# The reciprocal deviations of four normalisations: a power on GpSimd in place of a root on ScalarE and a reciprocal on VectorE

## The chip, the cores and the metric

The kernel runs on one core of a Trainium2 chip. The metric is the device time of one execution in microseconds, the median of the timed runs. The core's engines work side by side, each on its own queue in program order, and wait for each other by semaphores: PE (TensorE), VectorE (DVE), ScalarE (ACT), GpSimd (POOL) and SyncE (SP), which issues most of the DMAs.

## The reference

Two transformer layers with modulated normalisation, on x of 16 x 256 tokens (4096 in all) of width 128. In each layer, with six modulation vectors made from c:

    h = layernorm(x) * (1 + ca) + sa;  x = x + ga * attention(h)
    h = layernorm(x) * (1 + cb) + sb;  x = x + gb * feedforward(h)
    layernorm(x) = (x - mean) / sqrt(var + 1e-5), over the 128 features

The first layer's attention is a linear state-space scan with 16 states; its feed-forward is a mixture of 8 experts, two for each token, computed densely with rerouting by a similarity matrix. The second layer has causal attention with 16 heads, rotary embedding and relative positions; its feed-forward is a shared expert plus two of eight experts for each token, of hidden width 512. So there are four normalisations, numbered 0 to 3.

## The kernel before

The 4096 tokens are 32 tiles of 128 rows (`NT`), four tiles are a chunk of 512 (`NC` = 8 chunks), which is two sequences. X stays in SBUF for the whole kernel. Every engine has its instruction list written out by hand in the order in which it is to work; there is no planner. A wait at the head of an engine's list holds everything behind it.

A normalisation goes so: VectorE makes mean and variance of a chunk into `MV` (`statistics`, L1020, semaphore `s_mv`); ScalarE makes the deviation `SD` as `Sqrt(var + EPS)` (`s_sd`); VectorE takes the reciprocal into `RSTD`; then each tile is shifted and scaled, PE transposes it and ScalarE or VectorE applies the modulation into `hT`.

- Normalisation 0 (start): VectorE interleaves `first_statistics` and `normalise0` (L1064 to L1078); ScalarE makes six deviations before the first `features0`. After it VectorE makes the gates `GG`, which are stored and loaded again, broadcast, and GpSimd adds the attention's constant part to X (L652).
- Normalisation 1 (around 48 to 99 us): PE makes `outputs(c)` and, from c = 3, `transposes0(1, c - 3)` in turn (L1739). VectorE's loop (L1141) does `gated(c)`, `statistics(c - 1)`, `scales0(c - 2)`; GpSimd adds the residual between the first two. Here ScalarE normalises:

```python
            for c in range(NC):
                deviation(1, c)
                if c >= 2:
                    normalise1st(c - 2)
                if c >= 3:
                    features0(1, c - 3)
```

- Normalisation 2 (around 276 to 311 us): it follows the last expert pass of the first layer. For each chunk GpSimd makes a product with the gate (two halves, L675) and adds it to X (L679), VectorE makes the statistics behind it. One `Sqrt` over all 32 tiles (L769) and one reciprocal (L1102) follow, then `normalise(2)`.
- Normalisation 3 is spread over the second attention's eight pairs of sequences. `statistics1(i - 2)` comes at the end of pair i on VectorE. ScalarE makes the deviations in three lots: chunks 0 to 4 at the start of the last pair, 5 and 6, and 7 (L907); VectorE takes the reciprocals in the same lots (L1406) before `normalise1(0)`, `normalise1(5)` and `normalise1(7)` (L1394).

After the attention comes the tail, from about 660 to 815 us. For each of four groups of two chunks VectorE chooses the experts (`choose`) and computes destinations (`destinations`), and GpSimd scatters the rows with 16 indirect DMAs (L741). Beside that PE works through the shared expert (`shared_up`, `shared_down`), and VectorE adds its results (`shared_out`). The end of VectorE's list is: `destinations(2)`, `last_context(7)`, `shared_out(0)`, `gate_out(7)`, `last_residual(7)`, `statistics1(7)`, `shared_out(1)`, reciprocal, `normalise1(7)`, `shared_out(2)`, `choose(3)`, `shared_out(3)`, `destinations(3)`. PE's list has `norm_transposes(7)` behind `shared_up(3)`, then `shared_down(2)`, the router for chunk 7, and the rest of the shared blocks: `shared_up` 4 to 7 and `shared_down` 3 to 7. The routed experts' 39 tiles start when the shared expert and all scatters are done.

GpSimd's list in full: constant addition, residuals of layer 0 attention, a memset of `ACC`, the residuals of normalisation 2, rotary sums and low parts (L686, L691), for each pair `context`, `residual1` and copies (`neighbours`), then the four groups of scatters, then the results' scatters.

Of the kernel before, what the change touches and what calls it, by code (L numbers as in the profile page):

```python
# [19 lines left out]
ALU = mybir.AluOpType  # L20
# [3 lines left out]
P = 128  # L24
# [49 lines left out]
def build(nc, A, out):  # L74
    ctx = ExitStack()
    with ctx:
        def sb(name, shape, dt=F32):
            return ctx.enter_context(nc.sbuf_tensor("sb_" + name, shape, dt))
# [21 lines left out]
        MV = sb("MV", [P, NT, 2])  # L100
        RSTD = sb("RSTD", [P, NT])
        SD = sb("SD", [P, NT])
        NB = sb("NB", [P, NT])
        XN = sb("XN", [P, 2, TPC, D])
        epsc = sb("epsc", [P, 1])
        TMP = sb("TMP", [P, 2, CH])
# [179 lines left out]
        s_set = sem("s_set")  # L286
        s_cm = sem("s_cm")
        s_mod = sem("s_mod")
        s_gg = sem("s_gg")
        s_gst = sem("s_gst")  # L290
        s_gld = sem("s_gld")
        s_dv = sem("s_dv")
        s_mv = sem("s_mv")
        s_sd = sem("s_sd")
        s_xn = sem("s_xn")
# [349 lines left out]
        def _(pool):  # L645

            nc.gpsimd.memset(ones[:, :], 1.0).then_inc(s_set, 1)
            pool.wait_ge(s_vb, 16)
            pool.wait_ge(s_xn, NC)
# [12 lines left out]
            for c in range(NC):  # L662
                residual(c, c)
            nc.gpsimd.memset(ACC[:, :, :], 0.0).then_inc(s_zero, 1)
            pool.wait_ge(s_zero, 1)
# [3 lines left out]
            for c in range(NC):  # L669
                pool.wait_ge(s_acc[0], (E - 1) * NC + c + 1)  # L670
                t4 = TMP[:, c % 2, :].rearrange("p (b t f) -> p b t f", b=2, t=2)
                a4 = ACC[:, c * TPC:(c + 1) * TPC, :].rearrange("p (b t) f -> p b t f", b=2)
                for b in range(2):
                    gate = GATE[:, 1, 2 * c + b, :].unsqueeze(1).to_broadcast([P, 2, D])
                    ins = nc.gpsimd.tensor_tensor(t4[:, b], a4[:, b], gate, ALU.mult)  # L675
                ins.then_inc(s_gt0, 1)
                pool.wait_ge(s_gt0, c + 1)
                xs = X[:, c * TPC:(c + 1) * TPC, :].rearrange("p t f -> p (t f)")
                nc.gpsimd.tensor_tensor(xs, xs, TMP[:, c % 2, :], ALU.add).then_inc(s_r0, 1)  # L679

# [37 lines left out]
            for i in range(NP):  # L719
                if i == NP - 1:  # L720
                    nc.gpsimd.memset(RT1[32:33, :, :], 1.0).then_inc(s_one, 1)
                    pool.wait_ge(s_one, 1)
                if i >= 2:
                    context(i - 2)
                    residual1(i - 2)
                neighbours(i)
                pool.wait_ge(s_nb, 2 * i + 2)
            context(NP - 2)
            residual1(NP - 2)

            pool.wait_ge(s_pad, 16 * (E + 1))
            for g in range(GROUPS):
                pool.wait_ge(s_ids, 1 + (g > 0))
                pool.wait_ge(s_rows, 2 * GC * (g + 1))
# [25 lines left out]
        def _(act):  # L761
# [3 lines left out]
            def layer_norm(n, then=None):  # L765

                l, first = n // 2, 3 * (n % 2)
                act.wait_ge(s_mv, (n + 1) * NC)
                nc.scalar.activation(SD[:, :], MV[:, :, 1], ACT.Sqrt, bias=epsc[:, :]).then_inc(s_sd, 1)  # L769
                for c in range(NC):  # L770
# [9 lines left out]

            def deviation(n, c):
                act.wait_ge(s_mv, n * NC + c + 1)
                ts = slice(c * TPC, (c + 1) * TPC)
                nc.scalar.activation(SD[:, ts], MV[:, ts, 1], ACT.Sqrt, bias=epsc[:, :]).then_inc(s_sd, 1)

            def features0(n, c):
# [7 lines left out]

            for c in range(6):
                deviation(0, c)
            act.wait_ge(s_md, 1)
            features0(0, 0)
            features0(0, 1)
            deviation(0, 6)  # L800
            features0(0, 2)
            deviation(0, 7)
            def steps0(h):
# [30 lines left out]
            for c in range(NC):  # L834
                deviation(1, c)
                if c >= 2:
                    normalise1st(c - 2)
                if c >= 3:
                    features0(1, c - 3)
# [63 lines left out]
            exponentials(0)  # L903
            def deviations(n, lo, hi):
                act.wait_ge(s_mv, 3 * NC + hi)
                ts = slice(lo * TPC, hi * TPC)
                nc.scalar.activation(SD[:, ts], MV[:, ts, 1], ACT.Sqrt, bias=epsc[:, :]).then_inc(s_sd, 1)  # L907

            for i in range(1, NP):
                if i == NP - 1:  # L910
                    deviations(3, 0, 5)
                values_out(i - 1)
                relative_out(i - 1)
                exponentials(i)
# [43 lines left out]
            relative_out(NP - 1, (0,))  # L958
            deviations(4, 5, 7)
            shares(1)  # L960
# [10 lines left out]
            for c in range(3):  # L971
                shared_hidden(c)
            deviations(5, 7, 8)
            shared_hidden(3)
# [34 lines left out]
        def _(dve):  # L1009
# [18 lines left out]

            v.memset(epsc[:, :], EPS)
            for i in range(8):  # L1030
                link(v.memset(bank[i][:, :], 0.0))
            def normalise0(n, c):
                dve.wait_ge(s_sd, n * NC + c + 1)
                ts = slice(c * TPC, (c + 1) * TPC)
                link(v.reciprocal(RSTD[:, ts], SD[:, ts]))
                wait(dve, s_tr, n * NC + c - 1)
# [6 lines left out]
            def scales0(c):  # L1043
                dve.wait_ge(s_sd, NC + c + 1)
                ts = slice(c * TPC, (c + 1) * TPC)
                link(v.reciprocal(RSTD[:, ts], SD[:, ts]))
                v.scalar_tensor_tensor(out=NB[:, ts], in0=MV[:, ts, 0], scalar=-1.0, in1=RSTD[:, ts],
                                       op0=ALU.mult, op1=ALU.mult).then_inc(s_nbm, 1)
# [51 lines left out]
            def normalise(n, then=None):  # L1100
                dve.wait_ge(s_sd, n + 15)
                link(v.reciprocal(RSTD[:, :], SD[:, :]))  # L1102
                for c in range(NC):
                    wait(dve, s_tr, n * NC + c - 1)
                    for t in range(TPC):
# [287 lines left out]

            def normalise1(c):  # L1394
                if c >= 2:
                    dve.wait_ge(s_tr, 3 * NC + c - 1)
# [4 lines left out]
                ins.then_inc(s_xn, 1)  # L1401

            def inverse_deviations(n, lo, hi):
                dve.wait_ge(s_sd, n + 15)
                ts = slice(lo * TPC, hi * TPC)
                link(v.reciprocal(RSTD[:, ts], SD[:, ts]))  # L1406

            def last_pair(i, k):
# [6 lines left out]
                row_maxima(i, 1)  # L1415
                inverse_deviations(3, 0, 5)
                dve.wait_ge(s_wm[1], 16 * 11)
# [135 lines left out]
            statistics1(6)  # L1553
            inverse_deviations(4, 5, 7)
            normalise1(5)
# [13 lines left out]
            shared_out(1)  # L1569
            inverse_deviations(5, 7, 8)  # L1570
            normalise1(7)
# [725 lines left out]
```

## Time and profile before

| | before |
|---|---|
| median of 3 timed runs | 961.08 us (956.97 to 962.22) |
| span of the profiled execution | 1008.9 us |
| time of the profiled execution beside its span | none is given |
| PE busy | 838.6 us (83%) |
| VectorE busy | 592.7 us (59%) |
| ScalarE busy | 371.3 us (37%) |
| GpSimd busy | 255.6 us (25%) |
| mean granted TensorE clock | 0.890 of full |

The profile is of one execution, and its span is longer than the timed median. Times in it count from the first instruction. An engine is busy while one of its instructions executes, not while it waits. The chain is the work that ended last, followed back from the end through what released each step. Engines are named there PE, PEld (weight loads), DVE, ACT, POOL and SP; PEclk is the granted TensorE clock as a share of full.

### The profile page before, as it was taken

The numbers are of one execution on the slowest core, as the hardware profiler recorded it, in microseconds if no ns is written. First come the engines' busy times: TensorE is split into PE (matmuls) and PEld (weight loads), VectorE is DVE, ScalarE is ACT, GpSimd is POOL, SyncE is SP. The second block draws the span as 40 slices with busy tenths as digits, with TensorE's granted clock in tenths as the row PEclk, the third lists the DMA queues.
The fourth block names the chain that finished last, engine by engine and source line by source line (L and its number), as shares of the span: only waits on it lengthen the run. The fifth ranks groups of instructions, "written<-read, shape, count | busy, mean of one in ns | idle before, by whom it ended". The sixth has DMA issues, their size and how long they took to land.

```text
span 1008.9 us, 22593 instructions
## 1 busy us (share of the span) xinstructions
PE 838.6 (83%) x8710; PEld 572.5 (57%) x8710; DVE 592.7 (59%) x1638; ACT 371.3 (37%) x719; POOL 255.6 (25%) x252
## 2 busy tenths in 40 slices
PE   5545698999958789999999999986679789999960
PEld 3443365656634446656656656553257578888850
DVE  8632866666688787687687687763245232222217
ACT  3335221222214105435435436553325324444424
POOL 0522000000073601012011112034661514444440
PEclk9956699999989958999999999997688779999985
DMA  5600022226414761133233332121310417777746
GB/s 147 268 3 0 1 92 92 92 92 211 140 49 140 233 174 48 29 95 89 46 94 60 74 94 62 31 59 34 86 41 9 131 55 213 212 220 215 212 130 223
DMA packets 107827, 108.37 MB, mean 107 GB/s; under 512 B 48892, under 2 KB 93644, under 8 KB 106796
## 3 DMA queue, kind: packets, MB, share of 16 engines
q1 hardware_dynamic: 103196, 97.82, 33.7%
q0 software_dynamic: 4544, 9.35, 2.6%
q8 instruction: 60, 0.98, 0.4%
q14 instruction: 27, 0.22, 0.1%
HBM read 82.15 MB, written 44.78 MB: 126 GB/s over the span
## 4 chain that ended last, share of the span: by engine, by line
PE 62%; DVE 18%; issue 7%; ACT 5%; POOL 3%; DMA 3%; SPq 2%; POOLq 0%; DVEq 0%; ACTq 0%
PE bank L2148 8%; PE bank L2158 7%; PE bank L1928 7%; PE bank L1762 5%; PE bank L1773 5%; PE bank L1774 4%; PE bank L1868 4%; DVE sb_arena L1360 4%; PE bank L2077 3%; PE bank L1820 3%; PE bank L2067 3%; PE bank L1846 3%; DVE sb_ST L1023 2%; DVE sb_arena L1350 2%; DVE sb_arena L1352 2%
## 5 line engine op out<-in xcount | busy, mean ns | idle before, releaser
L1360 DVE TRANSPOSE_TENSOR_REDUCE sb_arena<-bank 128x16 f32<-128x512 f32 x192 | 120.3, 685 | 25.4 <-PE bank L1868 24.2
L901 ACT ACTIVATE sb_arena<-bank 128x512 f32<-128x512 f32 x192 | 99.2, 602 | 50.0 <-PE bank L1868 50.0
L989 ACT ACTIVATE sb_arena<-bank,sb_arena 128x256 f32<-128x256 f32 x156 | 65.3, 471 | 99.9 <-PE bank L2148 99.1
L749 POOL DMA_INDIRECT expert_results<-sb_arena x78 | 74.7, 958 | 105.5 <-DVE sb_arena L1619 88.9
L1762 PEld LDWEIGHTS bank<-sb_arena 128*128 128x128 f32 x512 | 67.9, 195 | 42.1 <-issue 25.3
L858 ACT ACTIVATE sb_arena<-bank 128x512 f32<-128x512 f32 x64 | 38.2, 597 | 143.9 <-PE bank L1774 143.8
L2148 PE MATMUL bank<-sb_arena 128*128 128x256 f32 x312 | 80.3, 402 | 3.8 <-DVE sb_arena L1615 1.8
L1928 PE MATMUL bank<-sb_arena 128*16 128x128 f32 x1024 | 71.9, 422 | 9.5 <-issue 9.4
L1762 PE MATMUL bank<-sb_arena 128*128 128x128 f32 x512 | 70.2, 281 | 10.5 <-DVE sb_arena L1192 10.5
L741 POOL DMA_INDIRECT dispatched_rows<-sb_arena x64 | 63.0, 984 | 62.7 <-DVE sb_arena L1525 44.4
L2158 PE MATMUL bank<-sb_arena 128*128 128x128 f32 x624 | 75.9, 275 | 0.0
L1254 DVE SCALAR_TENSOR_TENSOR sb_arena<-bank,sb_arena 128x128 f32<-128x128 f32 x256 | 71.7, 343 | 2.0 <-PE bank L1762 2.0
L2158 PEld LDWEIGHTS bank<-sb_arena 128*128 128x128 f32 x624 | 72.8, 192 | 0.1
L1192 DVE TENSOR_TENSOR sb_arena<-sb_arena,bank 128x512 f32<-128x512 f32 x64 | 43.7, 685 | 49.6 <-ACT sb_arena L858 49.0
L1773 PE MATMUL bank<-sb_arena 128*128 128x512 f32 x128 | 69.0, 622 | 0.0
L1774 PE MATMUL bank<-sb_arena 128*128 128x512 f32 x128 | 67.5, 609 | 0.0
L2148 PEld LDWEIGHTS bank<-sb_arena 128*128 128x128 f32 x312 | 58.3, 197 | 15.5 <-issue 5.3
L1820 PE MATMUL bank<-sb_arena 128*128 128x56 bf16 (+1 forms) x512 | 62.2, 281 | 5.5 <-DVE sb_arena L1340 3.2
L1350 DVE CAST sb_arena<-bank 128x512 bf16<-128x512 f32 x64 | 43.7, 682 | 37.0 <-PE bank L1820 37.0
L1613 DVE CAST sb_arena<-sb_arena 128x2 uint32<-128x2 f32 x39 | 7.8, 200 | 97.9 <-DMA expert_results<-sb_arena 81.3
L1868 PE MATMUL bank<-sb_arena,sb_identb 128*32 128x128 bf16 (+1 forms) x2304 | 63.1, 242 | 0.4 <-DVE sb_arena L1350 0.4
L1846 PE MATMUL bank<-sb_arena 32*128 32x256 bf16 x512 | 52.9, 285 | 6.8 <-DVE sb_arena L1360 4.5
(263 smaller groups left out, 1356.5 us busy)
## 6 DMA issues: line engine op xcount, KB each, us to landing
sb_arena<-in_w SPq DMA_DIRECT2D x39, 578.0 KB
dispatched_rows<-in_padding SPq DMA_DIRECT2D x8, 2064.0 KB, 9.5
sb_arena<-dispatched_rows SPq DMA_DIRECT2D x39, 129.0 KB
sb_arena<-q_parts SPq DMA_DIRECT2D x8, 512.0 KB, 5.5
sb_arena<-k_parts SPq DMA_DIRECT2D x8, 512.0 KB, 7.0
context_rel<-sb_arena SPq DMA_DIRECT2D x256, 8.0 KB
sb_arena<-expert_results SPq DMA_DIRECT2D x16, 256.0 KB, 5.9
q_parts<-sb_arena SPq DMA_DIRECT2D x24, 128.0 KB, 2.4
```

Source lines behind the costliest of these rows:

```text
L749: nc.gpsimd.indirect_dma_start(yD[:, :], bass.IndirectOffsetOnAxis(ap=rid[:, k, r:r + 1], axis=0), YS[:, k, r, :], None).then_inc(s_yo[k], 16)
L901: nc.scalar.activation(dst, src, ACT.Exp).then_inc(s_ex, 1)
L1360: v.tensor_reduce(dst.rearrange("p h b -> p (h b)"), bank[r % RING][:, :].rearrange("p (b c) -> p b c", c=32), AX, ALU.max, apply_transpos ...
L1762: ins = mm(bank[4 + j % 2][:, t * D:(t + 1) * D], HM0[:, j % 2, t * P:(t + 1) * P], W0[:, k, 2 * F0:3 * F0], start=True, stop=True)
L1773: mm(bank[j % 2][:, :], W0[:, k, 0:F0], chunk(hT, c), start=True, stop=True)
L1774: mm(bank[2 + j % 2][:, :], W0[:, k, F0:2 * F0], chunk(hT, c), start=True, stop=True).then_inc(s_up[0], 1)
L1820: ins = mm(out[:, :, :, x], GT4[:, first:first + 32, :].rearrange("p x a -> p (x a)"), queries[:, :, :, q], start=True, stop=True, skip_gr ...
L1846: mm(dst[:, x * S:(x + 1) * S], KG[k][rows, g, 0:P], QG[k][rows, g, :], start=(x == 0), stop=False, skip_group_check=True)
L1868: ins = mm(dst[32 * b:32 * b + 32, :, 32 * b:32 * b + w], identb[:, 32 * a:32 * a + 32], src[:, :, :].rearrange("p (g b) q -> p g b q", g= ...
L1928: ins = mm(out[32 * j:32 * j + 2 * HD, :, x], relk[:, 32 * j + 8 * w + 2 * x:32 * j + 8 * w + 2 * x + 2, :], four, start=True, stop=True, ...
L2148: ins = mm(bank[2 * (k % 2) + b // 2][:, b % 2 * GT:(b % 2 + 1) * GT], W1[:, k, b * P:(b + 1) * P], XT[:, k % 2, :], start=True, stop=True ...
L2158: ins = mm(bank[6 + k % 2][:, r * D:(r + 1) * D], HMT[:, k % 2, b, r * P:(r + 1) * P], W1[:, k, I1 + b * D:I1 + (b + 1) * D], start=(b == ...
```

## The change

The deviations leave ScalarE and the reciprocals leave VectorE. GpSimd computes, per chunk of four tiles, `SD = var + EPS` and then `RSTD = SD ** -0.5` with a tile of constants. VectorE's `inverse_deviation` is now only the wait for it. Normalisations 2 and 3 go by single chunks instead of lots. In GpSimd's queue the pairs stand behind the work that is shown here; the waits are part of that queue.

```diff
+            nc.gpsimd.memset(mhalf[:, :], -0.5).then_inc(s_half, 1)
+            pool.wait_ge(s_half, 1)
+            def inverse_deviation(n, c):
+                pool.wait_ge(s_mv, n * NC + c + 1)
+                ts = slice(c * TPC, (c + 1) * TPC)
+                nc.gpsimd.tensor_scalar(SD[:, ts], MV[:, ts, 1], EPS, None, ALU.add).then_inc(s_ve, 1)
+                pool.wait_ge(s_ve, n * NC + c + 1)
+                nc.gpsimd.tensor_tensor(RSTD[:, ts], SD[:, ts], mhalf[:, :], ALU.pow).then_inc(s_sd, 1)
+            for c in range(NC):
+                inverse_deviation(0, c)
...
             for c in range(NC):
                 residual(c, c)
+                if c:
+                    inverse_deviation(1, c - 1)
+            inverse_deviation(1, NC - 1)
...
                 nc.gpsimd.tensor_tensor(xs, xs, TMP[:, c % 2, :], ALU.add).then_inc(s_r0, 1)
+                if c:
+                    inverse_deviation(2, c - 1)
+            inverse_deviation(2, NC - 1)
...
+                if i >= 3:
+                    inverse_deviation(3, i - 3)
                 if i >= 2:
                     context(i - 2)
                     residual1(i - 2)
...
             context(NP - 2)
             residual1(NP - 2)
+            inverse_deviation(3, NP - 3)
+            inverse_deviation(3, NP - 2)
             pool.wait_ge(s_pad, 16 * (E + 1))
             for g in range(GROUPS):
+                if g == GROUPS - 1:
+                    inverse_deviation(3, NP - 1)
```

On ScalarE:

```diff
             def layer_norm(n, then=None):
-                act.wait_ge(s_mv, (n + 1) * NC)
-                nc.scalar.activation(SD[:, :], MV[:, :, 1], ACT.Sqrt, bias=epsc[:, :]).then_inc(s_sd, 1)
...
-            for c in range(6):
-                deviation(0, c)
             act.wait_ge(s_md, 1)
-            features0(0, 0)
-            features0(0, 1)
-            deviation(0, 6)
-            features0(0, 2)
-            deviation(0, 7)
+            for c in range(3):
+                features0(0, c)
...
             for c in range(NC):
-                deviation(1, c)
                 if c >= 2:
                     normalise1st(c - 2)
...
-                if i == NP - 1:
-                    deviations(3, 0, 5)
...
-            deviations(4, 5, 7)
...
-            deviations(5, 7, 8)
```

On VectorE:

```diff
+            def inverse_deviation(n, c):
+                dve.wait_ge(s_sd, n * NC + c + 1)
...
             def normalise0(n, c):
-                dve.wait_ge(s_sd, n * NC + c + 1)
-                ts = slice(c * TPC, (c + 1) * TPC)
-                link(v.reciprocal(RSTD[:, ts], SD[:, ts]))
+                inverse_deviation(n, c)
...
             def normalise(n, then=None):
-                dve.wait_ge(s_sd, n + 15)
-                link(v.reciprocal(RSTD[:, :], SD[:, :]))
                 for c in range(NC):
+                    inverse_deviation(n, c)
...
             def normalise1(c):
+                inverse_deviation(3, c)
...
-                inverse_deviations(3, 0, 5)
...
-            inverse_deviations(4, 5, 7)
...
-            inverse_deviations(5, 7, 8)
```

`scales0` loses its reciprocal as `normalise0` does. `epsc` and its memset go; `mhalf`, a tile of 128x4, comes.

## Rows read from the trace of the kernel before

**Rows 1.** The page: span and instructions; the chain that ended last, by engine.
```profile
span 1008.9 us, 22593 instructions
...
PE 62%; DVE 18%; issue 7%; ACT 5%; POOL 3%; DMA 3%; SPq 2%; POOLq 0%; DVEq 0%; ACTq 0%
```

**Rows 2.** Chain that ended last, 60 to 69 us: start us, us, what.
```profile
60.08 0.76 DVE sb_TMP L1119 x2
...
62.26 1.64 ACT sb_XN L830 x4
...
63.95 1.11 PE bank L1665 x4
...
68.51 0.75 DVE sb_TMP L1119 x2
```

**Rows 3.** Timelines of VectorE and ScalarE, second normalisation: start us, us, what, [idle before].
```profile
53.96 0.16 DVE L1047 SCALAR_TENSOR_TENSOR sb_NB<-sb_MV,sb_RSTD 128x4 f32<-128x4 f32 x1
...
62.06 0.30 ACT L784 ACTIVATE sb_SD<-sb_MV,sb_epsc 128x4 f32<-128x4 f32 x1 [6.33 <-DVE sb_MV L1026]
...
84.54 0.76 DVE L1119 TENSOR_TENSOR sb_TMP<-bank,sb_GATE 128x256 f32<-128x256 f32 x2 [5.44 <-PE bank L1716]
```

**Rows 4.** Timelines of GpSimd and VectorE in the tail.
```profile
675.59 1.17 POOL L741 DMA_INDIRECT dispatched_rows<-sb_arena  x1 [2.45 <-DVE sb_arena L1525]
...
755.44 1.31 POOL L741 DMA_INDIRECT dispatched_rows<-sb_arena  x1 [0.30 <-issue]
...
676.37 0.38 DVE L1026 BATCH_NORM_AGGREGATE sb_MV<-sb_ST 128x2 f32<-128x6 f32 x4
...
742.72 0.76 DVE L1472 TENSOR_TENSOR sb_arena<-bank,sb_GATE 128x256 f32<-128x256 f32 x2 [2.07 <-issue]
...
745.14 0.38 DVE L1026 BATCH_NORM_AGGREGATE sb_MV<-sb_ST 128x2 f32<-128x6 f32 x4
...
753.71 0.69 DVE L1529 TENSOR_TENSOR sb_arena<-bank,sb_arena 128x512 f32<-128x512 f32 x1 [8.19 <-remote]
...
755.84 0.17 DVE L1406 RECIPROCAL sb_RSTD<-sb_SD 128x4 f32<-128x4 f32 x1
```

**Rows 5.** Four windows from 683 to 801 us, and their sum: busy us, PEclk.
```profile
683.00:698.00 15.00, 5.73 (x34) 1.68 (x33) 7.22 (x31) 4.98 (x7) 9.67 (x11) 0.66 0.15 48
...
sum 55.00, PE 24.11 PEld 8.34 DVE 10.40 ACT 10.29 POOL 34.07; mean PE 6.03 PEld 2.08 DVE 2.60 ACT 2.57 POOL 8.52
```

**Rows 6.** Timeline of PE in the tail.
```profile
698.22 2.31 PE L1928 MATMUL bank<-sb_arena 128*16 128x128 f32 x33 [1.03 <-issue]
...
710.83 5.40 PE L2067 MATMUL bank<-sb_arena 128*128 128x512 f32 x8
...
742.46 3.74 PE L2077 MATMUL bank<-sb_arena 128*128 128x128 f32 x32
...
758.12 5.95 PE L2077 MATMUL bank<-sb_arena 128*128 128x128 f32 x32
...
801.37 9.80 PE L2077 MATMUL bank<-sb_arena 128*128 128x128 f32 x61 [0.35 <-issue]
```

**Rows 7.** First normalisation: VectorE's timeline, then one window of all engines.
```profile
10.94 0.15 DVE L1035 RECIPROCAL sb_RSTD<-sb_SD 128x4 f32<-128x4 f32 x1
...
9.80:27.40 17.60, 13.14 (x65) 9.28 (x68) 17.06 (x95) 7.70 (x20) 0.00 (x0) 0.85 0.30 79
```

**Rows 8.** GpSimd's instructions grouped by line: busy us, mean ns | idle before, releasers.
```profile
L741 POOL DMA_INDIRECT dispatched_rows<-sb_arena x64 | 63.0, 984 | 62.7 <-DVE sb_arena L1525 44.4 <-issue 18.0 <-DMA dispatched_rows<-sb_arena 0.3
```

**Rows 9.** Timelines of GpSimd and VectorE, third normalisation.
```profile
275.83 1.42 POOL L675 TENSOR_TENSOR sb_TMP<-sb_arena,sb_GATE 128x256 f32<-128x256 f32 x2 [185.75 <-DVE sb_arena L1254]
...
297.32 1.26 POOL L679 TENSOR_TENSOR sb_X<-sb_X,sb_TMP 128x512 f32<-128x512 f32 x1
...
300.68 2.14 DVE L1107 TENSOR_SCALAR sb_XN<-sb_X,sb_MV,sb_RSTD 128x128 f32<-128x128 f32 x8
```

**Rows 10.** Groups of ScalarE's instructions by line: the table loads at one line.
```profile
L907 ACT ACT_TABLE_LOAD x3 | 3.8, 1283 | 0.1
```

More of the change, by code:

```diff
@@ L101, in build @@
         RSTD = sb("RSTD", [P, NT])
+        NB = sb("NB", [P, NT])
         SD = sb("SD", [P, NT])
-        NB = sb("NB", [P, NT])
+        mhalf = sb("mhalf", [P, TPC])
         XN = sb("XN", [P, 2, TPC, D])
-        epsc = sb("epsc", [P, 1])
         TMP = sb("TMP", [P, 2, CH])
@@ L287, in build @@
         s_cm = sem("s_cm")
+        s_mv = sem("s_mv")
+        s_sd = sem("s_sd")
+        s_ve = sem("s_ve")
+        s_half = sem("s_half")
         s_mod = sem("s_mod")
@@ L292, in build @@
         s_dv = sem("s_dv")
-        s_mv = sem("s_mv")
-        s_sd = sem("s_sd")
         s_xn = sem("s_xn")
@@ L779, in layer_norm @@
                         then(c)
-            def deviation(n, c):
-                act.wait_ge(s_mv, n * NC + c + 1)
-                ts = slice(c * TPC, (c + 1) * TPC)
-                nc.scalar.activation(SD[:, ts], MV[:, ts, 1], ACT.Sqrt, bias=epsc[:, :]).then_inc(s_sd, 1)
             def features0(n, c):
@@ L903, in _ @@
             exponentials(0)
[L904 to L907, printed above, removed]
             for i in range(1, NP):
-                if i == NP - 1:
-                    deviations(3, 0, 5)
                 values_out(i - 1)
@@ L1027, in statistics @@
                 ins.then_inc(s_mv, 1)
-            v.memset(epsc[:, :], EPS)
+            def inverse_deviation(n, c):
+                dve.wait_ge(s_sd, n * NC + c + 1)
             for i in range(8):
@@ L1032, in normalise0 @@
             def normalise0(n, c):
-                dve.wait_ge(s_sd, n * NC + c + 1)
-                ts = slice(c * TPC, (c + 1) * TPC)
-                link(v.reciprocal(RSTD[:, ts], SD[:, ts]))
+                inverse_deviation(n, c)
                 wait(dve, s_tr, n * NC + c - 1)
@@ L1043, in scales0 @@
             def scales0(c):
-                dve.wait_ge(s_sd, NC + c + 1)
+                inverse_deviation(1, c)
                 ts = slice(c * TPC, (c + 1) * TPC)
-                link(v.reciprocal(RSTD[:, ts], SD[:, ts]))
                 v.scalar_tensor_tensor(out=NB[:, ts], in0=MV[:, ts, 0], scalar=-1.0, in1=RSTD[:, ts],
@@ L1401, in normalise1 @@
                 ins.then_inc(s_xn, 1)
[L1403 to L1406, printed above, removed]
             def last_pair(i, k):
```

## The prediction

> **What bounds the kernel now.** I read the page first, then the chain that ended last, then the timelines of the four normalisations engine by engine. The span is 1008.9 us and PE carries 62% of the chain, VectorE 18% [rows 1]. So an edit of GpSimd and ScalarE counts only where PE stands waiting for them. There are four places to look at, one per normalisation.
>
> In the second normalisation the chain goes round ScalarE once per chunk. VectorE multiplies by the gate (0.76 us) and makes statistics, ScalarE takes the root and then normalises an older chunk (1.64), PE transposes it (1.11) and only then makes the next outputs, which take from 65.06 to 68.5 at this clock [rows 2]. Three such turns lead from the gate at 60.08 to that at 84.54, 8.15 us each [rows 2, 3]. The thing to see is the order on ScalarE: `deviation(1, c)` stands in its queue ahead of `normalise1st(c - 2)`. The scales for chunk 1 were done at 54.12, but its normalisation started at 62.26, behind the root of chunk 3, which had waited 6.33 us for statistics [rows 2, 3]. That is head-of-line blocking, not work.
>
> In the tail, GpSimd issues the dispatch scatters in four bursts of 16; the first starts at 675.59, the third ends at 756.75 [rows 4]. Late in each burst PE has nearly nothing to do: it is busy 24.1 of 55 us in four windows, so 30.9 us go idle, and its clock in the first of them is 0.66 of full [rows 5].
>
> How the profiled execution stands to the runs: its span is 47.8 us above the median of 961.08. No other time of it is given, so the sum is made against the span and its difference laid on the median. Where those 47.8 us lie decides one term, so I made an account of the tail: every instruction at its measured length, without the pauses of [rows 5]. From 683.3 the 34 PE records of the first window take 2.4 us at 0.07 each, and what stands from 698.22 to 710.83 takes its 12.6: the shared hidden layer starts at 698.3 [rows 5, 6]. Four blocks at 3.74, the ranks (0.6) and the last projection (1.05) end at 714.9. VectorE needs about 1 more for the first shared output, 2.8 for gate, residual and statistics (742.72 to 745.52) and 2.1 for the second shared output (753.71 to 755.84): chunk 7 could be normalised at 720.8 where the trace has 756.05 [rows 4]. PE then has a transpose and the router (about 4) and ten blocks of 3.74, ending near 762 where the trace has 811.2 [rows 6]. That is 49 us, against 47.8 missing. I take it that most of the pauses are absent from the timed runs. It is an inference from one sum; its failure is a rival below.
>
> **The change part by part.**
>
> First normalisation: eight reciprocals leave VectorE, 0.15 us each and 0.03 to the next start. VectorE is busy 17.06 of the 17.6 us up to 27.4 [rows 7], and the gates, their transfer and the first GpSimd additions hang on its end: 8 x 0.18 = -1.5 us. GpSimd has nothing to do there, which hides the new operations; each is wanted 2 us or more after its statistics.
>
> The price of one pair on GpSimd, x: the trace shows no power. An addition of 128x512 takes 1.26 us and two products of 128x256 take 1.42 [rows 9], so 0.16 us for 128x4 by the line through them; the handoff between the two is 0.08. The power lies between another such operation (0.16) and the dearest GpSimd instruction here, a scatter of 1.31 us [rows 4]. I take 0.5, nearer the small one, because its size is that row's. So x = 0.75, ends 0.4 and 1.55.
>
> Second normalisation: the root leaves ScalarE's queue, so `normalise1st(c)` needs only `scales0(c)`. The loop gate, statistics, scales, normalise, transpose, outputs is still 8.2 us long but spans two chunks: the outputs of chunk c+1 follow a transpose that depends on the gate of chunk c-1. PE's own part of a turn, about 0.9 + 3.4 = 4.3 us at this clock, becomes the bound; at the upper clock it is about half and the loop gives 3.3. Step by step: chunk 0 is normalised at 51.85, not behind the third root at 54.10; the gate at 60.08 comes at 57.8; three turns then take 12.9 or 9.9 us, and the last gate is at 70.7 or 67.7 instead of 84.54. After it ScalarE has one chunk less to normalise, 2.6 us. Gain 16.4 to 19.5. PE is busy enough to rise part way: -18.3. GpSimd idles some 6 us a chunk there, which hides x up to 2.5 us.
>
> Third: here GpSimd is full. From 275.83 to 298.58 it works 21.8 of 22.75 us on residuals [rows 9]. Six pairs now stand ahead of the last residual: 6x less the 1.0 idle. After it the last statistics no longer go through ScalarE and a reciprocal of 32 columns, from 299.9 to 300.68 [rows 9]: -0.8. Net 6x - 1.75 = +2.75, ends +0.65 and +7.55.
>
> Last attention pair: one reciprocal, about 0.3 with its hop, leaves the chain, and a table load of 1.28 [rows 10] no longer delays the exponentials, of which I count 0.3: -0.6. In the attention pairs the new operations lie in GpSimd's idle time.
>
> A rule speaks to those loads. The Trainium skill, "ScalarE: Activation LUTs", section on table sets, says to group calls by set, since each switch needs a load of about 1283 ns. The trace agrees with the length [rows 10]. Ten of nineteen loads would go, an estimate of 12.8 us if each counted; by the trace nearly all stand ahead of a wait, so the sum has them only as above.
>
> Tail: two waits are new. The first burst now stands behind `inverse_deviation(3, 6)`, whose statistics end at 676.75 [rows 4], and starts at 677.55, +1.96. And `inverse_deviation(3, 7)` stands in GpSimd's queue behind the whole third burst. Queued behind `normalise1(7)` on VectorE are the shared outputs, `choose(3)` and the last destinations; on PE, `norm_transposes(7)` stands ahead of ten blocks. In the profile that costs little: chunk 7 at 757.6 instead of 756.05, +1.5. Without the pauses it costs much. A scatter takes (63.0 + 18) / 64 = 1.27 us with its gap [rows 8], the 18 being the gaps of 0.30; a burst 20.2. Three of them back to back from 677.55 end at 738.8 (their destinations are ready by 693 and 707 in the account), so chunk 7 is normalised at 739.6 instead of 720.8: +18.8. PE, idle that long, comes back at its lower clock; the first block after the gap took 5.95 instead of 3.74 [rows 6], +2.2 and a little more: +2.7. Tail +21.5.
>
> Sum: -1.5 - 18.3 + 2.75 - 0.6 + 21.5 = +3.9: 1012.8 against the span by this account, 965 us on the median.
>
> **The rivals.**
>
> A. The pauses are in the timed runs too. The tail then costs 1.5 and a little, and the sum is -15: 946 us. For it: they are in the trace, and the trace names no cause. Against it: the account of 49 us. 
>
> B. The wait is there but shorter: bursts run faster untraced, or chunk 7 is ready after 720.8 because its context first crosses memory. At 17 us a burst it shrinks by 10: tail +11, 955 us. It decides between this and the forecast whether three bursts take over 58 us.
>
> C. Slower: GpSimd is the bound of the third normalisation and x is dear. At x = 1.25 that term is +5.75, the two pairs of the tail add 1, and the sum is +7.9: 969 us; from x = 0.9 on, the rest as forecast, the kernel ends slower by over 0.5%. Each microsecond more costs eight.
>
> D. ScalarE's queue was not what held the second stage. Against it are the 6.33 us and the start 0.2 after the root. The sum would be +22: 983 us.
>
> **How the numbers follow.** The forecast has 0.38: 965, its own range 960 to 969. A has 0.22, B 0.18, C 0.20, D 0.02. The range reaches to A's 946 and past C's 969 to 971, leaving out half of A, D and a dear power: 2 in 10. A measurement tells 0.5% here, 4.8 us. Faster is A, two thirds of B and a little of the forecast's low side, 0.37; same is most of the forecast and the rest of B, 0.34; slower is C, D and the forecast's upper end, 0.29.
>
> **What would show it.** In the new profile: no root on ScalarE; the gates of chunks 4 to 7 at turns of 3.3 to 4.3 us; the spacing of GpSimd's small operations, giving x; in the third normalisation GpSimd without gaps and VectorE waiting for it; the first burst after the seventh pair; the eighth pair right behind the third burst with `normalise1(7)` waiting for it. The profiled span may well fall by 15 us while the timed median does not. Wrong would be: an x over 2.5 us, turns still near 8 us, or a timed gain of 10 us and more, which would mean that the wait in the tail is not there.

## The result, and the profile after

The changed kernel takes 970.86 us (median of 4 runs, 967.86 to 974.39), the kernel before 961.65 on the same chip: a ratio of 1.0109, 95% interval 1.0073 to 1.0146. Two later comparisons, on two chips, gave 1.0076 (1.0044 to 1.0108) and 1.0080 (1.0050 to 1.0110). So it is slower by 0.8 to 1.1%. The forecast was +0.35%, inside what a measurement can tell from nothing, with "faster" as the likeliest sign; the time lay inside the range, the sign did not come out as weighed.

The page of the changed kernel answers to [rows 1]: its span, and the shares of the chain that ended last. GpSimd has gone from 3% to 10% (from 5% by the later profile of before that has no pauses).

```profile
span 966.0 us, 22619 instructions
...
PE 52%; DVE 20%; POOL 10%; DMA 7%; issue 6%; ACT 3%; SPq 2%; POOLq 0%; DVEq 0%
```

Its groups of instructions by line show the price that no row of before had. The columns are busy us, mean ns of one | idle before.

```profile
L659 POOL TENSOR_TENSOR sb_RSTD<-sb_SD,sb_mhalf 128x4 f32<-128x4 f32 x32 | 33.2, 1038 | 2.7
...
L657 POOL TENSOR_SCALAR sb_SD<-sb_MV 128x4 f32<-128x4 f32 x32 | 7.5, 235 | 20.2 <-DVE sb_MV L1031 19.9
```

A power of 128x4 takes 1.04 us and not 0.5; an addition of 128x512 takes 1.26 on the same engine, the addition of EPS to the same 128x4 tile 0.235. No small two-input operation of another kind was run, so that it is the power that costs, and not the form of the instruction, rests on the prediction's line through the additions and products (0.16 for 128x4).

The second normalisation is what [rows 2, 3] were for. VectorE's timeline, start us, us, what, [idle before]:

```profile
56.75 0.76 DVE L1123 TENSOR_TENSOR sb_TMP<-bank,sb_GATE 128x256 f32<-128x256 f32 x2 [3.05 <-PE bank L1713]
...
58.97 0.76 DVE L1123 TENSOR_TENSOR sb_TMP<-bank,sb_GATE 128x256 f32<-128x256 f32 x2
...
63.09 0.75 DVE L1123 TENSOR_TENSOR sb_TMP<-bank,sb_GATE 128x256 f32<-128x256 f32 x2 [1.66 <-PE bank L1713]
...
65.65 0.76 DVE L1123 TENSOR_TENSOR sb_TMP<-bank,sb_GATE 128x256 f32<-128x256 f32 x2 [0.43 <-PE bank L1713]
```

The gates of the last four chunks come after turns of 2.2, 4.1 and 2.6 us, where it was 8.15 each, and the last is at 65.65 instead of 84.54.

In the third normalisation GpSimd's timeline has no gap:

```profile
257.35 0.23 POOL L657 TENSOR_SCALAR sb_SD<-sb_MV 128x4 f32<-128x4 f32 x1
257.66 1.04 POOL L659 TENSOR_TENSOR sb_RSTD<-sb_SD,sb_mhalf 128x4 f32<-128x4 f32 x1
258.67 1.42 POOL L693 TENSOR_TENSOR sb_TMP<-sb_arena,sb_GATE 128x256 f32<-128x256 f32 x2
260.17 1.26 POOL L697 TENSOR_TENSOR sb_X<-sb_X,sb_TMP 128x512 f32<-128x512 f32 x1
261.40 0.23 POOL L657 TENSOR_SCALAR sb_SD<-sb_MV 128x4 f32<-128x4 f32 x1
```

From one addition of EPS to the next are 4.05 us; the pair has 1.32 of them (257.35 to 258.67). At the last chunk's statistics VectorE waits 2.74 us for GpSimd's addition:

```profile
281.67 0.87 DVE L1028 BATCH_NORM_STATS2 sb_ST<-sb_X 128x6 f32<-128x128 f32 x4 [2.74 <-POOL sb_X L697]
```

And the tail, the timelines of GpSimd, VectorE and PE. The eighth pair stands right behind the last scatter of the third burst, chunk 7's statistics are 21 us old by then, and VectorE and PE stand idle:

```profile
723.56 0.96 POOL L768 DMA_INDIRECT dispatched_rows<-sb_arena  x1 [0.30 <-issue]
724.56 0.25 POOL L657 TENSOR_SCALAR sb_SD<-sb_MV 128x4 f32<-128x4 f32 x1
724.90 1.05 POOL L659 TENSOR_TENSOR sb_RSTD<-sb_SD,sb_mhalf 128x4 f32<-128x4 f32 x1
...
702.69 0.38 DVE L1031 BATCH_NORM_AGGREGATE sb_MV<-sb_ST 128x2 f32<-128x6 f32 x4
...
725.98 1.11 DVE L1404 TENSOR_SCALAR sb_arena<-sb_X,sb_MV,sb_RSTD 128x128 f32<-128x128 f32 x4 [19.98 <-POOL sb_RSTD L659]
...
727.15 1.12 PE L1951 MATMUL bank<-sb_ident,sb_arena 128*128 128x128 f32 x4 [19.97 <-DVE sb_arena L1404]
728.06 5.46 PE L2074 MATMUL bank<-sb_arena 128*128 128x128 f32 x32
```

The first block after the gap takes 5.46 us, with a granted clock of 0.64 of full from 727 to 733.4 us, those after it 3.73, at 1.00.

### The profile page after: what moved, and what is told of

It is laid out like the page before. It is cut to its first block, busy times and chain, and to the rows that moved or that the text cites. A ratio compares the mean times of both kernels' runs of the same rounds, so it can differ in the third digit from the quotient of the medians.

```text
span 966.0 us, 22619 instructions
## 1 busy us (share of the span) xinstructions
PE 817.1 (85%) x8710; PEld 561.1 (58%) x8710; DVE 591.7 (61%) x1617; ACT 354.5 (37%) x689; POOL 295.6 (31%) x317
## 4 chain that ended last, share of the span: by engine, by line
PE 52%; DVE 20%; POOL 10%; DMA 7%; issue 6%; ACT 3%; SPq 2%; POOLq 0%; DVEq 0%
PE bank L1925 7%; PE bank L2145 5%; PE bank L1759 5%; PE bank L2155 5%; PE bank L1770 5%; POOL dispatched_rows L768 5%; PE bank L1771 5%; DVE sb_arena L1364 5%; PE bank L1865 4%; PE bank L1817 4%; DMA expert_results<-sb_arena 3%; PE bank L1843 3%; DVE sb_arena L1354 2%; DVE sb_arena L1356 2%; DVE sb_ST L1028 2%
## 5 line engine op out<-in xcount | busy, mean ns | idle before, releaser
L2145 PE MATMUL bank<-sb_arena 128*128 128x256 f32 x312 | 78.0, 394 | 4.9 <-DVE sb_arena L1612 4.2
L1925 PE MATMUL bank<-sb_arena 128*16 128x128 f32 x1024 | 68.1, 423 | 0.0
L1770 PE MATMUL bank<-sb_arena 128*128 128x512 f32 x128 | 68.0, 613 | 0.0
L1771 PE MATMUL bank<-sb_arena 128*128 128x512 f32 x128 | 66.5, 602 | 0.0
L693 POOL TENSOR_TENSOR sb_TMP<-sb_arena,sb_GATE 128x256 f32<-128x256 f32 x16 | 11.3, 729 | 177.9 <-DVE sb_arena L1258 177.9
```

What stands on the lines that cost most here:

```text
L1770: mm(bank[j % 2][:, :], W0[:, k, 0:F0], chunk(hT, c), start=True, stop=True)
L1771: mm(bank[2 + j % 2][:, :], W0[:, k, F0:2 * F0], chunk(hT, c), start=True, stop=True).then_inc(s_up[0], 1)
L1925: ins = mm(out[32 * j:32 * j + 2 * HD, :, x], relk[:, 32 * j + 8 * w + 2 * x:32 * j + 8 * w + 2 * x + 2, :], four, start=True, stop=True, ...
L2145: ins = mm(bank[2 * (k % 2) + b // 2][:, b % 2 * GT:(b % 2 + 1) * GT], W1[:, k, b * P:(b + 1) * P], XT[:, k % 2, :], start=True, stop=True ...
```

## The experiments

**The kernel before, profiled again.** No edit. The whole account of the tail hung on pauses that only the one profile of before had shown [rows 5], so this came first.

> The kernel before, unchanged, profiled once more. By my account the pauses of GpSimd's scatters and of PE in the tail belong to the one profiled execution: the span is then 955 to 962 us, within 3 us of the time of its own run, the shared hidden layer starts near 698 us and chunk 7 is normalised near 720.8 us. If the pauses belong to every execution that is profiled, the span is again near 1009 us. If the timed runs hold them too (rival A), a profile without them would show a time well under the median of 961.65 us.

It took 1012.38 us and its span was 1010.5: the pauses are there, and they do not come from profiling alone, since the kernel before took 1013.97 us (median of 11 runs) on this chip, and 960.71, 961.22 and 962.09 on the three others of the experiments. The chips differ, or their state in those minutes does: all the runs of these experiments on it were timed together, so no run tells the two apart. That it was one profiled execution, as the prediction put it, is wrong; that the runs shown had no pauses was still open. So it was profiled once more, on another chip:

> The kernel before, profiled a third time, in the hope of a chip on which it takes 961 us. If so, the account of the tail in the prediction can be read against a trace: shared hidden layer at 698 us, chunk 7 normalised at 720.8 us, PE's shared blocks ended near 762 us, span 952 to 963 us. On a chip where it takes 1014 us, the pauses are there again and it tells nothing new.

961.44 us, span 959.6, no pauses. Timelines of VectorE and PE of this third profile:

```profile
720.54 1.12 DVE L1399 TENSOR_SCALAR sb_arena<-sb_X,sb_MV,sb_RSTD 128x128 f32<-128x128 f32 x4
...
759.79 2.06 PE L2077 MATMUL bank<-sb_arena 128*128 128x128 f32 x17
...
765.89 0.41 PE L2139 MATMUL bank<-sb_ident,sb_arena 128*128 128x128 f32 x2 [4.04 <-DMA sb_arena<-dispatched_rows]
```

The account had chunk 7 normalised at 720.8 and PE's blocks ended near 762; the trace has 720.54 and 761.85 (759.79 and 2.06). This profile, not that of [rows 1], is the one to hold against the changed kernel's.

**One edit in the tail.** On the chip with pauses first, then on one without:

```diff
             for g in range(GROUPS):
-                if g == GROUPS - 1:
+                if g == GROUPS - 2:
                     inverse_deviation(3, NP - 1)
```

> The changed kernel, with the eighth pair of the last normalisation put ahead of the third burst of scatters instead of the fourth. By the forecast's step for the tail: the statistics of chunk 7 were done at 703.07 us and the second shared output at 705.99 us, the second burst ends at 704.1 us, so chunk 7 is normalised at about 706 instead of 725.98 us and the end comes 20 us sooner, or a little more for PE's clock: 948 to 952 us against the 970.86 of the changed kernel. If the wait behind the third burst is not what costs (the bursts themselves, or the rows that they write, hold the expert tiles), nothing or only a few us are gained: 966 to 971 us.

997.67 us where the kernel before took 1013.97, ratio 0.9864 (0.9825 to 0.9903). The numbers expected were for the other kind of chip and can't be read here.

> The changed kernel with the eighth pair ahead of the third burst, again. Where the kernel before takes 961 us: the same edit took 23.5 us off the version with the third normalisation as before (960.56 to 937.05), so if the two costs are independent it comes to 944 us here too (941 to 947), against 968 to 971 for the changed kernel. If the third normalisation's delay had been hidden by the wait, less than 20 us come off. On a chip with pauses the ratio to the kernel before is again 0.986.

> The changed kernel a third time, for its ratio beside the kernel above on one chip. Where the kernel before takes 961 us the ratio is 1.008 to 1.011. Where it takes 1014 us with pauses in the bursts, rival A's case holds: the eighth pair waits little longer than its statistics do, and the ratio is 0.983 to 0.990, near that of the kernel above.

948.66 us against 970.29 for the changed kernel and 962.09 for the kernel before, all on one chip: 21.6 us from one line that moves two instructions of 1.3 us together (941 to 947 us were expected, so it missed by 1.7). The ratio to before is 0.9852 (0.9810 to 0.9893). GpSimd's timeline shows the pair now between the bursts, with VectorE's wait down to under 1 us:

```profile
709.04 0.26 POOL L657 TENSOR_SCALAR sb_SD<-sb_MV 128x4 f32<-128x4 f32 x1
709.39 1.47 POOL L659 TENSOR_TENSOR sb_RSTD<-sb_SD,sb_mhalf 128x4 f32<-128x4 f32 x1
...
710.89 1.34 DVE L1404 TENSOR_SCALAR sb_arena<-sb_X,sb_MV,sb_RSTD 128x128 f32<-128x128 f32 x4 [0.94 <-POOL sb_RSTD L659]
```

**The second normalisation alone.** The kernel before, with the pairs on GpSimd for that one; `scales0` has no reciprocal then, which the cut below leaves out:

```diff
             for c in range(NC):
                 residual(c, c)
+                if c:
+                    inverse_deviation(1, c - 1)
+            inverse_deviation(1, NC - 1)
...
             for c in range(NC):
-                deviation(1, c)
                 if c >= 2:
                     normalise1st(c - 2)
```

> The kernel before, with the pairs on GpSimd for the second normalisation alone. If the root in ScalarE's queue held that stage, the gates of chunks 4 to 7 come at turns of 2 to 4 us and the whole gain of about 20 us, less the 2 that seem to be given back in the expert stage, stays: 940 to 944 us against 961.65. If the gain in that stage is taken back later (the expert stage or PE's clock), it ends over 950 us.

On the chip with pauses: 996.79 us, 0.9846 (0.9804 to 0.9888).

> The kernel before with the pairs of the second normalisation alone on GpSimd, again. Where the kernel before takes 961 us: the trace of the changed kernel has 21.9 us less up to the first exponential of the router and 22.4 at the first residual of the third normalisation, first normalisation taken off, so 937 to 941 us. If the other edits took part in that gain, over 945 us.

On one without: 941.57 us, 0.9775 (0.9729 to 0.9821), 19.7 us less than the kernel before.

**The order alone.** The kernel before, one line moved on ScalarE; GpSimd gets nothing:

```diff
             for c in range(NC):
-                deviation(1, c)
                 if c >= 2:
                     normalise1st(c - 2)
                 if c >= 3:
                     features0(1, c - 3)
+                deviation(1, c)
```

> The kernel before, with one line moved: in the second normalisation ScalarE takes the root of chunk c after it has normalised chunk c - 2 and made the features of chunk c - 3, not before. No work leaves ScalarE or VectorE. If head-of-line blocking was the whole cost, as the forecast said, this gains what moving the pairs to GpSimd gains, less the root and the reciprocal (0.3 + 0.2 us per chunk, partly hidden): 940 to 947 us. If it is the engine's load or the hops that cost (rival), it gains less than half of it: 952 to 962 us.

993.30 us with pauses, 0.9832 (0.9783 to 0.9881).

> The kernel before with the root of the second normalisation taken later in ScalarE's queue, again. Where the kernel before takes 961 us: its profile had the first exponential of the router at 82.93 us where the version on GpSimd had 79.91 and the kernel before 102.95 on the same chip, so it gains 20 us, 3 less than with GpSimd: 939 to 944 us. If ScalarE's work, not its order, was the cost, over 950 us.

946.37 us without, 0.9825 (0.9775 to 0.9875): 14.9 us less than before, though the runs spread from 937.19 to 948.40 and the two versions' intervals overlap. ScalarE's timeline in it answers to the second row of [rows 3]:

```profile
61.25 0.30 ACT L784 ACTIVATE sb_SD<-sb_MV,sb_epsc 128x4 f32<-128x4 f32 x1 [3.57 <-DVE sb_MV L1026]
61.51 1.65 ACT L830 ACTIVATE sb_XN<-sb_X,sb_NB,sb_RSTD 128x128 f32<-128x128 f32 x4
...
67.68 0.30 ACT L784 ACTIVATE sb_SD<-sb_MV,sb_epsc 128x4 f32<-128x4 f32 x1 [0.99 <-DVE sb_MV L1026]
```

The root still waits, but 3.57 and 0.99 us and not 6.33, and by then its engine has nothing else that is ready. In the profiles the first exponential of the router comes at 83.96 here, at 82.71 with GpSimd and at 102.62 in the kernel before. The 1.25 us between the first two are the length of a table load, which stands here ahead of that exponential and not in the version with GpSimd:

```profile
82.67 1.28 ACT L848 ACT_TABLE_LOAD   x1
83.96 0.31 ACT L848 ACTIVATE sb_arena<-sb_arena 128x128 f32<-128x128 f32 x1
```

So by the traces nearly all of the gain in this stage was the order. By the times it was at least three quarters (14.9 of 19.7 us here, and 20.7 against 17.2 on the chip with pauses). The 946.37 lies 2 us over the range that was expected.

**The last normalisation alone.** The kernel before, with the pairs of that one placed as in the changed kernel:

```diff
             for g in range(GROUPS):
+                if g == GROUPS - 1:
+                    inverse_deviation(3, NP - 1)
...
             shared_out(1)
-            inverse_deviations(5, 7, 8)
             normalise1(7)
```

> The kernel before with the pairs of the last normalisation alone on GpSimd, in the places of the changed kernel. Where the kernel before takes 961 us: with the first, second and last normalisation changed it took 960.56 us, the first two are worth 1.5 and 22, so the last costs 23: 981 to 986 us (the forecast had 21 for it). If the tail's cost arises only because the second stage's gain brings the bursts nearer to their destinations (an interplay), it costs less alone: 965 to 975 us. On a chip with pauses in the bursts it costs 0 to 5 us.

986.75 us, 1.0245 (1.0199 to 1.0291): 25.5 us more. In its trace VectorE waits 21.41 us for the eighth pair. No interplay is needed.

```profile
746.22 1.11 DVE L1416 TENSOR_SCALAR sb_arena<-sb_X,sb_MV,sb_RSTD 128x128 f32<-128x128 f32 x4 [21.41 <-POOL sb_RSTD L660]
```

**The third normalisation as before,** in the changed kernel, alone and with the eighth pair moved:

```diff
                 nc.gpsimd.tensor_tensor(xs, xs, TMP[:, c % 2, :], ALU.add).then_inc(s_r0, 1)
-                if c:
-                    inverse_deviation(2, c - 1)
-            inverse_deviation(2, NC - 1)
...
                 l, first = n // 2, 3 * (n % 2)
+                if n == 2:
+                    act.wait_ge(s_mv, (n + 1) * NC)
+                    nc.scalar.activation(SD[:, :], MV[:, :, 1], ACT.Sqrt, bias=epsc[:, :]).then_inc(s_sd, 1)
...
             def normalise(n, then=None):
+                dve.wait_ge(s_sd, n + 15)
+                link(v.reciprocal(RSTD[:, :], SD[:, :]))
                 for c in range(NC):
-                    inverse_deviation(n, c)
```

> The changed kernel, unchanged, beside the kernel before on the same chip. Two kinds of executions are seen so far: the kernel before at 961 us, without pauses of PE during the bursts of scatters, and at 1014 us with them. If this chip is of the first kind, the ratio is again 1.011 (the wait of 20 us for the eighth pair costs in full). If it is of the second kind, GpSimd's third burst begins late enough in both kernels that the eighth pair waits for little, rival A's case: the changed kernel is then faster, by 12 to 17 us, a ratio of 0.983 to 0.988.

967.79 us, 1.0076 (1.0044 to 1.0108), on the chip of the three runs that follow. It has no pauses.

> The changed kernel with the third normalisation as before (one root on ScalarE, one reciprocal on VectorE). A pair measured 1.33 us from start to start, and GpSimd had no gap there, so six pairs less the 1.75 us that the change saved in that place are 6.2 us: 964 to 966 us where the changed kernel takes 970.9, on the other kind of chip the same 6 us less. By the forecast's price of 0.75 us a pair it would be 2.75 us, and if GpSimd did not set that stage, nothing.

960.56 us: 7.2 less than the changed kernel.

> The changed kernel with both costs taken out: the third normalisation as before, and the eighth pair of the last one ahead of the third burst instead of the fourth. If the two terms are what turned the gain of the second normalisation into a loss, and add up, 6 and 20 us come off where there are no pauses: 943 to 947 us beside 961 for the kernel before. With pauses in the bursts the second term is small, and it stands 5 to 8 us below the changed kernel. If they overlap, it is no better than the better one alone.

937.05 us, 0.9762 (0.9717 to 0.9806): 23.5 us less again. The two costs add up (30.7 us together, 7.2 and 21.6 alone), and without them the change is 2.4% faster than the kernel before. The range expected, 943 to 947, was too high by 6 us: it took the two from the 970.86 of the first chip, where this one has 967.79, and counted 20 for the pair.

**The price doubled.**

```diff
+                nc.gpsimd.tensor_tensor(twice[:, n, ts], SD[:, ts], mhalf[:, :], ALU.pow)
                 nc.gpsimd.tensor_tensor(RSTD[:, ts], SD[:, ts], mhalf[:, :], ALU.pow).then_inc(s_sd, 1)
```

> The changed kernel with every power on GpSimd made twice (the first into a tile of its own that nobody reads). Each pair costs 1.04 to 1.1 us more. By the forecast's account this is paid six to seven times in the third normalisation and twice in the tail and is hidden elsewhere: 8 to 9.5 us more than the changed kernel. If the pairs of the second normalisation are also on the path (they have 1.2 us of slack at this price), 12 to 16 us more. If GpSimd's time does not count, within 2 us.

980.60 us, 12.8 more than the changed kernel, its runs spread over 10 us. The two executions that were profiled differ by less, 976.25 against 970.61 us, so their traces can't hold all of the 12.8. They put chunk 7's last normalisation 7.3 us later (727.66 to 734.96). The third normalisation takes 5.8 more, its six powers. The router's first exponential comes 4.3 later. Of these, 2.7 are there at GpSimd's first addition: the pairs no longer fit into the first normalisation's slack, and VectorE waits 0.65 and 1.19 us for its last two. Before the third normalisation 1.7 of the 4.3 are gone again, and 1.7 more go between it and the first `normalise1`; only 0.7 comes in the tail, where the rule has two powers. So the forecast's rule, eight times the added 1.0 us, gives 8 and the traces have 7.3, but not made up as the rule has it, since it held the first two normalisations to be free. The medians have half as much again, inside the 12 to 16 us that were expected for the case in which the second normalisation pays too; no trace shows where.

## Why the prediction was wrong

The two profiles without pauses, 959.6 and 966.0 us of span (961.44 and 967.86 timed), allow a ledger. Each row is a mark on the path, its time before and after, and what the stretch up to it adds. Another profile of the changed kernel has its marks up to 1.9 us elsewhere (the first `normalise1` at 628.25, 628.38 and 630.01 us), so a single row is good to one or two microseconds.

| up to | before | after | adds | forecast |
|---|---|---|---|---|
| first addition on GpSimd | 36.98 | 35.57 | -1.4 | -1.5 |
| router's first exponential | 102.62 | 79.17 | -22.0 | -18.3 |
| first product of the third normalisation | 275.91 | 251.89 | -0.6 | |
| memset behind its normalisation | 309.79 | 292.36 | +6.6 | +2.75 |
| first `normalise1` | 645.84 | 628.25 | -0.2 | -0.6 |
| end of the shared blocks | 761.85 | 769.44 | +25.2 | +21.5 |
| end of the span | 959.6 | 966.0 | -1.2 | |

The rows behind four of them, of before (the third profile) and then of after:

```profile
102.62 0.31 ACT L848 ACTIVATE sb_arena<-sb_arena 128x128 f32<-128x128 f32 x1
...
275.91 1.42 POOL L675 TENSOR_TENSOR sb_TMP<-sb_arena,sb_GATE 128x256 f32<-128x256 f32 x2 [185.74 <-DVE sb_arena L1254]
...
309.79 1.02 DVE L1313 MEMSET sb_arena<- 128x1152 f32 x1 [0.19 <-issue]
```

```profile
79.17 0.31 ACT L862 ACTIVATE sb_arena<-sb_arena 128x128 f32<-128x128 f32 x1
...
251.89 1.42 POOL L693 TENSOR_TENSOR sb_TMP<-sb_arena,sb_GATE 128x256 f32<-128x256 f32 x2 [177.91 <-DVE sb_arena L1258]
...
292.36 1.02 DVE L1317 MEMSET sb_arena<- 128x1152 f32 x1 [0.19 <-issue]
...
762.13 7.31 PE L2074 MATMUL bank<-sb_arena 128*128 128x128 f32 x64
```

**The step that failed is the price of a pair.** The prediction took x = 0.75 us with a power at 0.5, because "its size is that row's", a small operation by the size of its tile. It measured 1.33, with a power at 1.04. The prediction had its own lever for this: eight microseconds of time per microsecond of x. 8 x 0.58 = 4.6 us on top of +3.9 is +8.5, and three comparisons have 1.0109, 1.0076 and 1.0080, or +7 to +10. Rival C, "x is dear", with x = 1.25 and 969 us, is what happened; it was given 0.20.

That 969 and 970.86 lie so near is in part luck. The ledger has +6.4 where the forecast has +3.9. The third normalisation costs 3.8 more than forecast, nearly all of it x. The tail costs 3.7 more, of which x has 1.2. The second normalisation gains 3.7 more, which hides the tail's error, and small terms have the rest. And the medians differ by 9.2 us where the two profiled executions differ by 6.4: the one of the changed kernel, 967.86, was the lowest of its four.

**Third normalisation.** 6x - 1.75 with the measured x is +6.2; the ledger has +6.6, and putting it back gained 7.2. The mechanism (GpSimd full, so every pair in the open) was right, the term was mis-sized by x alone.

**Second normalisation.** Head-of-line blocking was right: moving one line on ScalarE gained 14.9 us by itself. The size was low: -22.0, or -19.7 timed alone. The turns came at 2.2 to 4.1 us, not 3.3 to 4.3, and PE had reached its upper clock at 55.9 us: two matmuls of L1713 took 0.64 us up to there and 0.39 from there on, with a granted clock of 0.51 from 50 to 55.9 us and 1.00 from there to 60. In the third profile of before the granted clock was 0.51 to 0.68 from 50 to 90 us, and the same two matmuls still took 0.63 us at 76 us. The prediction had PE "rise part way"; it rose in full. So a part of the gain is PE's clock.

A load of a function table that stood between the copy of the logits and the first exponential is gone as well: from the start of the copy to that exponential were 1.90 us (100.72 to 102.62), and are 0.48 (78.69 to 79.17).

```profile
101.32 1.28 ACT L848 ACT_TABLE_LOAD   x1
```

That is 1.4 of the 22. On the prediction's sentence about the Trainium skill's rule ("ScalarE: Activation LUTs", table sets): 19 loads became 9, this is the one of the ten that stands on the chain of work in the profile of before, and it counted in full; the estimate of 12.8 us, each load counted, is too high.

**Tail.** VectorE's wait is there, 19.98 us of it; pulling the pair forward gained 21.6 and 23.5, and the last normalisation alone cost 25.5. By the ledger chunk 7 is normalised 23.0 us later than the stages ahead of it explain (720.54 to 725.98, and 17.6 taken off), where the forecast had 18.8.

Most of the difference lies ahead of the first burst. From the first `normalise1` to it were 29.87 us (645.84 to 675.71) and are 35.33 (628.25 to 663.58): 5.5 more, not 1.96. The wait for the seventh pair has 2.8 of it (destinations were ready at 660.6, and 0.2 us of issue stand ahead of a burst in any case): 1.4 until its statistics are done, and the pair. The other 2.7 are PE's clock, which the forecast did not have: from the transposes at 644.10 to those at 650.10 PE takes 6.00 us, where it took 3.31 (661.76 to 665.07).

The windows below, of after and then of the third profile of before, show these blocks (column PEclk, behind the five engines) at 0.52 and at 1.00 of full clock. The clock fell at 642.9, about 0.15 us after PE had gone idle at 642.78, behind 16 matmuls of 8 columns (L1983); it was back by 650. In before, PE went idle there behind the same kind of matmuls and the clock stayed. PE stood idle 1.33 us in the one and 1.12 in the other, but the clock was down before that difference could arise. The traces with the last normalisation changed all have that slow stretch, in whole or in part; so have, in part, those with only the second normalisation's order or pairs changed (`root_later_b`, `second_only`). Why the clock falls there is not settled.

```profile
644.00:650.00 6.00, 5.90 (x68) 2.98 (x68) 5.21 (x19) 1.75 (x4) 1.92 (x2) 0.52 0.46 137
```

```profile
661.00:667.00 6.00, 5.24 (x77) 3.01 (x78) 5.31 (x17) 3.44 (x8) 2.33 (x3) 1.00 0.54 146
```

After chunk 7's normalisation the tail takes 2.2 us more than before, where the forecast had 2.7 for PE's lower clock.

**First normalisation and last pair** came as forecast within 0.4 us.

Two small slips in the prediction's working change nothing. From 677.55, 48 scatters of 1.27 us end at 738.5 and not at 738.8. And GpSimd's busy time on the residuals is 21.34 of the 22.75 us by the profile's window, not 21.8; the last addition did start 7.0 us later (21.49 to 28.49 us behind the first product), which is six pairs less the 1.0 of idle.

**The pauses, rival A.** The inference from one sum (49 us against 47.8) was right in what it said of the runs, and wrong in where it put the pauses: not in one profiled execution, but in every run on one chip. On that chip the kernel before takes 1014 us run after run, GpSimd's third burst starts late, and rival A's premise holds. Moving the eighth pair forward gives 0.9864 there and 0.9852 elsewhere. The changed kernel itself was not run on it, so A's 946 (a gain of 15 us) stays open for that chip. It can't have been the case in the result, whose own trace has no pauses and has the wait of 19.98 us.

**B and D.** B wanted three bursts in under 58 us; they took 60.9 (663.58 to 724.5). Its other way, chunk 7 ready only after 720.8, did not come either: the third profile of before has it at 720.54. D is excluded by the moved line.

## What to carry to other kernels

Do not price an operation that no trace shows by the size of its tile alone (here a power of 128x4 took 1.04 us and an addition to the same tile 0.235); multiply the doubt by how often it stands in the open before choosing the likeliest value, and let the chances follow from that product. When work moves to another engine, walk down that engine's queue and ask of every new wait what stands ahead of it that is long: here two cheap instructions behind 16 scatters cost more than the whole second stage gave. And when a wait at the head of a queue is the cost, first try the other order on the same engine: it had at least three quarters of the gain for one moved line.

## What the hardware showed that I had not expected

On one of the four chips of the experiments PE all but stops for stretches of 16 us and less while GpSimd issues scatters. Its timeline in the kernel with the eighth pair moved:

```profile
672.34 0.37 PE L1925 MATMUL bank<-sb_arena 128*16 128x128 f32 x1 [0.30 <-issue]
673.05 0.37 PE L1925 MATMUL bank<-sb_arena 128*16 128x128 f32 x1 [0.33 <-issue]
673.76 0.38 PE L1925 MATMUL bank<-sb_arena 128*16 128x128 f32 x1 [0.34 <-issue]
674.48 0.38 PE L1925 MATMUL bank<-sb_arena 128*16 128x128 f32 x1 [0.34 <-issue]
675.86 0.43 PE L1925 MATMUL bank<-sb_arena 128*16 128x128 f32 x2 [1.01 <-issue]
```

One matmul each 0.71 us, or a few after a multiple of that, where elsewhere 32 take 2.2 us. In 16 us from 672 PE is busy 6.16 there, and 15.73 in the changed kernel's stretch from 664 to 680 on another chip. The scatters themselves keep their 1.27 us. No row names what PE waits for, and I did not find it.

VectorE's small product of means and reciprocals is held by GpSimd's additions. Two timelines of the changed kernel, of GpSimd and of VectorE:

```profile
52.42 1.27 POOL L675 TENSOR_TENSOR sb_X<-sb_X,sb_TMP 128x512 f32<-128x512 f32 x1
...
57.58 1.28 POOL L675 TENSOR_TENSOR sb_X<-sb_X,sb_TMP 128x512 f32<-128x512 f32 x1 [2.58 <-DVE sb_TMP L1123]
...
52.92 0.78 DVE L1052 SCALAR_TENSOR_TENSOR sb_NB<-sb_MV,sb_RSTD 128x4 f32<-128x4 f32 x1
...
58.62 0.26 DVE L1052 SCALAR_TENSOR_TENSOR sb_NB<-sb_MV,sb_RSTD 128x4 f32<-128x4 f32 x1
...
69.11 0.16 DVE L1052 SCALAR_TENSOR_TENSOR sb_NB<-sb_MV,sb_RSTD 128x4 f32<-128x4 f32 x1
```

It takes 0.16 us where no addition runs, and beside one it ends 0.01 or 0.02 us after it: at 53.70 behind the addition that ends at 53.69, and at 58.88 behind the one that ends at 58.86. The Trainium skill, "GPSIMD Engine Reference", section "Key points", says that the two engines share their way into SBUF and contend where VectorE reads two inputs from it; the trace agrees. The six of the eight products that start beside an addition take 0.26 to 0.94 us, so each lost 0.1 to 0.8. In the third profile of the kernel before all eight took 0.16 us.
